# Splitting the score maxima on GpSimd, and turning them one step later, in two 512-key attentions

## The chip, the cores and the metric

The kernel runs on one core of one Trainium2 chip. The time is the device time of one execution of the whole program in microseconds, as the median of several runs. Three runs of the kernel before took 1183.32, 1192.98 and 1194.06 us; the median is 1192.98 us.

## The reference

The program is a decoder of two layers over x of 4 sequences x 512 tokens x 128 channels (16 heads of 8 channels). It adds six blocks to x one after the other: an RWKV recurrence, a small cross attention, a dense path with mixture-of-experts, an attention with relative positions, a latent cross attention, and an attention with register tokens and two groups of keys. Two of these hold a full softmax attention of 512 queries against 512 keys for 64 heads (4 sequences x 16), and the change touches these two alone. Cut to that:

```
# dense path of the first layer ("da", causal)
scores = einsum('bqhd,bkhd->bhqk', q, k) / sqrt(hd)
scores = where(causal, scores, finfo.min)
o = einsum('bhqk,bkhd->bqhd', softmax(scores), v)
# last block ("ga", grouped keys): token q sees the keys of its own group
l = where(key_mask, einsum('bqhd,bkhd->bhqk', q * scale, k), -inf)
x_pos / x_neg = einsum('bhqk,bkhd->bqhd', softmax(l), v)
```

## The kernel before, in words

Both attentions are one function, `attention_stage`, called with the tag `da` (causal) and the tag `ga` (not causal). The 64 heads are taken four at a time, which makes 16 **units** (`QUADS`), and a unit has 8 **steps**, so 128 steps (`STEPS`). q and k are held as sums of bfloat16 parts, so that the score matmuls run in bfloat16.

In step `s` each engine has its own fixed list of work, in program order, and semaphores alone tie the lists together.

- **Scores.** TensorE computes the scores of two heads for 128 queries, queries on partitions (`scores`, L947), into one of two pairs of PSUM banks. In `da` eight small matmuls lower the masked square (`mask_scores`, L958). VectorE takes the negated row maxima (L1196). The scores of step s wait for the reduction of step s-2.
- **Maxima.** After the eighth step of a unit VectorE splits the 128 x 16 maxima into three bfloat16 parts in four small dependent instructions (`split_maxima`, L1181 to L1187). In the second step of the next unit (`step % 8 == 1`) TensorE turns the parts onto 12 rows (`turn_maxima`, L969), ScalarE copies them from PSUM to `mrows` (`copy_maxima`, L1108), and SP, or ScalarE for the first unit, sends two small DMAs into rows of `qst` (`load_maxima`, L838).
- **Turned scores.** `S_LAG` steps after a step's scores, TensorE computes the scores again with keys on partitions (`scores_t`, L983); the rows loaded above subtract the maximum inside the matmul. The first of a unit (r == 0) waits for the two DMAs. `S_LAG` is 14 in `da` and 13 in `ga`. The results and the turned maxima share a ring of three PSUM banks (`st_ring`, `wait_bank`).
- **Exponentials.** ScalarE takes exp of both heads (L1100) into `pt`. In `da` GpSimd zeroes the masked triangle (`affine_select`, L897).
- **Values.** `V_LAG` = 3 steps later TensorE multiplies `pt` with the values (`values`, L1002) into one bank for the unit. When a unit's eight are done, ScalarE copies the bank out (`copy_output`, L1120), and the first value matmul of the next unit waits for that copy.

TensorE's order in a step of `da` is: turned scores, scores, mask, values, and in one step of eight the turn of the maxima. In `ga` it is: scores, turned scores, values, turn. ScalarE's order is: exponentials, copy of the maxima, copy of the output. SP issues, for unit u, the maxima's two DMAs and then the loads of unit u+3 (L820), in one queue. After step 127 come the sums over heads, reciprocals and the output projections (`join`, `densify`, `output`, L1015 to L1027), some of them at fixed steps of the drain.

Of the kernel before, what the change touches and what calls it, by code (L numbers as in the profile page):

```python
# [21 lines left out]
ALU = mybir.AluOpType  # L22
# [677 lines left out]
QUADS = B * H // 4  # L700
STEPS = 8 * QUADS


def attention_stage(nc, g, tag, xn, wq, wk, wv, group, scale, o, wo, take, patch=None, causal=False, classes=None,
# [3 lines left out]
    KT = KS + 3  # L708
    NBUF, SLOTS = 4, 3
    S_GROUPS, ST_BANK, ST_BANKS, O_BANK = 2, 4, 3, 7  # L710
    S_LAG, V_LAG = 14 if causal else 13, 3
    GATE_STEP, ROUTE_STEPS, LOGIT_STEP = 24, 8, 10

    def first_query(kt):
        return kt * 128 if causal else 0

    def keys_of(qt):
        return (qt + 1) * 128 if causal else T
# [11 lines left out]
    st_ring, st_slot, turn_slot = [], {}, {}  # L730
    for step in range(STEPS + S_LAG):
        t = step - S_LAG
        if t >= 0:
            for par in range(2):
                st_slot[t, par] = len(st_ring)
                st_ring.append(("scores", 2 * t + par + 1))
        if step % 8 == 1 and 8 < step < STEPS + 8:
            turn_slot[step // 8 - 1] = len(st_ring)
            st_ring.append(("maxima", step // 8))

    def st_bank(slot):
        return ST_BANK + slot % ST_BANKS

    with ExitStack() as ctx:
# [8 lines left out]
        with ExitStack() as inner:  # L753
            def isb(name, shape, dt=fp32):
                return inner.enter_context(nc.sbuf_tensor(f"{tag}_{name}", shape, dt))
# [3 lines left out]
            pt = isb("pt", [128, SLOTS, 4, T])  # L759
            zero = isb("zero", [128, T])  # L760
            nmax = isb("nmax", [128, 2, 2, 2, QT])
            mrest = isb("mrest", [128, 2, 2, 2, QT])
            mparts = isb("mparts", [128, 2, QT, 2, 3, 2], bf16)
            mrows = isb("mrows", [12, 2, T], bf16)
# [5 lines left out]
            m_loaded = [sem(f"m_loaded_{n}") for n in range(2)]  # L770
# [18 lines left out]
            with nc.Block() as block:  # L789
# [89 lines left out]
                @block.gpsimd  # L879
                def _(pool):  # L880
                    nc.gpsimd.memset(kst[32:64, :, :, :], 1.0).then_inc(ones_set, 1)
                    nc.gpsimd.memset(kst[96:128, :, :, :], 1.0).then_inc(ones_set, 1)
                    pool.wait_ge(ones_set, 2)
                    nc.gpsimd.memset(zero[:, :], 0.0).then_inc(zeroed, 1)
                    nc.gpsimd.memset(v9[:, :, :, HD:HD + 1], 1.0).then_inc(one, 1)
                    if gates:
                        gates.clear(pool)
                    if front:
                        front.gpsimd(pool)
                    if causal:  # L890
                        for t in range(STEPS):
                            u, r = divmod(t, 8)
                            kt, pr = divmod(r, 2)
                            q0 = first_query(kt)
                            pool.wait_ge(exped, 2 * t + 2)
                            square = pt[:, (4 * u + kt) % SLOTS, 2 * pr:2 * pr + 2, q0:q0 + 128]
                            nc.gpsimd.affine_select(square, square, [[0, 2], [1, 128]], ALU.is_ge, 0.0, base=0,  # L897
                                                    channel_multiplier=-1).then_inc(selected, 1)
                    if finish:
                        finish.add(pool)  # L900

                @block.tensor
                def _(pe):
# [126 lines left out]
                    for step in range(ALL_STEPS):  # L1030
                        t = step - S_LAG
                        if causal and 0 <= t < STEPS:
                            scores_t(t)
                        if step < STEPS:
                            scores(step)
                            if causal:
                                mask_scores(step)
                        if not causal and 0 <= t < STEPS:
                            scores_t(t)
                        if 0 <= t - V_LAG < STEPS:  # L1040
                            values(t - V_LAG)
                        if step % 8 == 1 and step // 8 - 1 in turn_slot:
                            turn_maxima(step // 8 - 1)
                        if front and step < S_LAG:
                            front.registers_pe(pe, step)
                        if gates and step < ROUTE_STEPS:
                            gates.route(pe, step)
                        if front and step == S_LAG - 1:
                            clear_output()
                        if step in OUT_STEP:  # L1050
                            output(OUT_STEP[step])
                        if step in JOIN_STEP:
                            join(JOIN_STEP[step])
                            densify(JOIN_STEP[step])
                        if gates and step == S_LAG - 1:
                            pe.wait_ge(gates.copied, 1)
# [12 lines left out]
                def _(act):  # L1069
# [34 lines left out]
                    def copy_maxima(u):  # L1104
                        act.wait_ge(m_turned, u + 1)
                        if u >= 2:
                            act.wait_ge(m_loaded[u % 2], 32 * (u // 2))
                        nc.scalar.activation(mrows[:, u % 2, :], g.ps[0:12, st_bank(turn_slot[u]), :], ACT.Identity)\  # L1108
                            .then_inc(m_ready, 1)
# [15 lines left out]
                    for step in range(ALL_STEPS):  # L1125
                        t = step - S_LAG
                        if front and step < S_LAG:
                            front.registers_act(act, step)
                        if 0 <= t < STEPS:
                            exponentials(t)  # L1130
                        if step % 8 == 1 and step // 8 - 1 in turn_slot:
                            copy_maxima(step // 8 - 1)
                            if step // 8 == 1:
                                load_first_maxima()
                        if gates and step == GATE_STEP + 6:
                            gates.exp(act)
                        p = t - V_LAG
                        if p >= 0 and p % 8 == 7:
                            copy_output(p // 8)
                        if finish and step == ALL_STEPS - 2:  # L1140
                            act.wait_ge(taken, 1)
                            finish.square(act)
# [12 lines left out]
                def _(dve):  # L1155
# [16 lines left out]
                    else:  # L1172
                        split()

                    def split_maxima(u):
                        dve.wait_ge(maxed, 8 * (u + 1))
                        if u >= 2:
                            dve.wait_ge(m_turned, u - 1)
                        n = u % 2
                        part = lambda k: mparts[:, n, :, :, k, :].rearrange("p q a r -> p a r q")  # L1180
                        nc.vector.tensor_copy(part(0), nmax[:, n]).then_inc(split1, 1)  # L1181
                        dve.wait_ge(split1, u + 1)
                        nc.vector.tensor_tensor(mrest[:, n], nmax[:, n], part(0), ALU.subtract).then_inc(split2, 1)
                        dve.wait_ge(split2, u + 1)
                        nc.vector.tensor_copy(part(1), mrest[:, n]).then_inc(split3, 1)
                        dve.wait_ge(split3, u + 1)
                        nc.vector.tensor_tensor(part(2), mrest[:, n], part(1), ALU.subtract).then_inc(split4, 1)  # L1187

                    chain = gates.chain(dve) if gates else None
                    for step in range(STEPS):  # L1190
                        u, r = divmod(step, 8)
                        pr, qt = divmod(r, 4)
                        if gates and (step == LOGIT_STEP or step >= GATE_STEP):
                            next(chain, None)
                        dve.wait_ge(scored, step + 1)
                        nc.vector.tensor_reduce(nmax[:, u % 2, :, pr, qt],  # L1196
                                                g.ps[:, 2 * (step % S_GROUPS):2 * (step % S_GROUPS) + 2, 0:keys_of(qt)],
                                                AX.X, ALU.max, negate=True).then_inc(maxed, 1)
                        if r == 7:
                            split_maxima(u)  # L1200
                        if front and step < S_LAG:
                            front.registers_dve(dve, step)

                    def invert(b):
                        dve.wait_ge(summed, b + 1)
# [1850 lines left out]
```

## Time and profile before

| what | value |
|---|---|
| median of three runs | 1192.98 us |
| profiled execution, its own time | 1189.37 us |
| its span in the trace | 1187.6 us |
| PE busy / DVE / ACT / POOL, share of the span | 92% / 68% / 61% / 29% |
| mean granted TensorE clock | 0.968 |
| stage `da`, steps 0 to 127 of the maxima | 156.2 to 296.5 us |
| stage `ga`, steps 0 to 127 of the maxima | 992.6 to 1154.9 us |

PE is TensorE's matmuls, PEld its weight loads, DVE VectorE, ACT ScalarE, POOL GpSimd, SP the queue that issues DMAs. Times in the views are microseconds from the start of the span. A row of the timeline merges neighbouring instructions of one line; "x8" is their number and the second figure the time from the first start to the last end. Brackets give the idle time of that engine before the row and what ended it.

### The profile page before, as it was taken

How to read it: one execution, taken by the hardware profiler on the slowest of the kernel's cores; microseconds unless marked ns; L12 is line 12 of the kernel's file. 1: busy time of each engine (PE TensorE's matmuls, PEld its weight loads, DVE VectorE, ACT ScalarE, POOL GpSimd, SP SyncE). 2: the span in 40 equal slices, each digit the busy share in tenths (PEclk: the TensorE clock that was granted, in tenths of full speed). 3: DMA queues.
4: the chain of work that ended last, by engine and by line, in shares of the span. 5: the costliest groups of instructions: out<-in, count | busy, mean ns of one | idle time of the engine just before them, and what ended most of it. 6: DMA issues, size and time to landing. Idle time of an engine off the chain costs nothing. (4 is left out here: it accounts for less than half of the span.)

```text
span 1187.6 us, 35597 instructions
## 1 busy us (share of the span) xinstructions
PE 1097.9 (92%) x14750; PEld 562.0 (47%) x14750; DVE 810.4 (68%) x1312; ACT 729.9 (61%) x1464; POOL 340.4 (29%) x667
## 2 busy tenths in 40 slices
PE   6999899999899998889999999999988888899997
PEld 2344443333244443567767767766745333222222
DVE  4897478888533443377767767777716466999995
ACT  5313637888554434466675766666744373899994
POOL 0552203333235244333333224322113431100000
PEclk9999869999999999899999999999989997999999
DMA  5000054211093200601021021101100003511100
GB/s 203 1 0 1 8 153 150 57 45 31 4 183 76 71 1 0 125 14 10 8 20 10 8 17 10 11 8 9 11 6 1 1 14 83 202 44 44 44 17 36
DMA packets 134927, 51.61 MB, mean 43 GB/s; under 512 B 103968, under 2 KB 126512, under 8 KB 134256
## 3 DMA queue, kind: packets, MB, share of 16 engines
q1 hardware_dynamic: 134732, 49.32, 17.8%
q8 instruction: 118, 1.93, 0.7%
q14 instruction: 41, 0.34, 0.1%
q10 hardware_dynamic: 36, 0.02, 0.0%
HBM read 33.09 MB, written 15.81 MB: 41 GB/s over the span
## 5 line engine op out<-in xcount | busy, mean ns | idle before, releaser
L2489 DVE TENSOR_REDUCE re_nmax<-ps 128x1 f32<-128x512 f32 x256 | 159.0, 683 | 57.9 <-PE ps L2292 57.9
L2423 ACT ACTIVATE normed<-ps,re_nmax 128x512 f32<-128x512 f32 x256 | 154.9, 693 | 4.7 <-DVE re_nmax L2489 4.7
L2313 PE MATMUL ps<-const,normed 128*128 128x128 f32 x1024 | 147.0, 283 | 2.5 <-ACT normed L2423 2.2
L1100 ACT ACTIVATE ga_pt<-ps 128x512 f32<-128x512 f32 x256 | 139.2, 598 | 15.4 <-PE ps L983 13.8
L2429 ACT ACTIVATE re_pT<-ps 128x512 f32<-128x512 f32 x128 | 76.6, 599 | 116.2 <-PE ps L2313 116.0
L1196 DVE TENSOR_REDUCE ga_nmax<-ps 128x2 f32<-128x1024 f32 x128 | 146.7, 1216 | 1.4 <-PE ps L947 1.4
L2313 PEld LDWEIGHTS ps<-const,normed 128*128 128x128 f32 x1024 | 110.4, 142 | 28.7 <-issue 14.9
L1196 DVE TENSOR_REDUCE da_nmax<-ps 128x2 f32<-128x256 f32 (+3 forms) x128 | 102.9, 821 | 20.7 <-PE ps L958 18.8
L1100 ACT ACTIVATE da_pt<-ps 128x512 f32<-128x512 f32 (+3 forms) x256 | 96.7, 435 | 31.6 <-PE ps L983 28.9
L2509 DVE COPY re_pT<-ps 128x512 f32<-128x512 f32 x128 | 82.5, 685 | 34.1 <-PE ps L2313 34.1
L1659 DVE TENSOR_TENSOR ex_u<-ps,ex_s 128x512 f32<-128x512 f32 x48 | 32.8, 690 | 90.9 <-PE ps L1494 68.0
L1002 PE MATMUL ps<-ga_pt,ga_v 128*9 128x256 f32 x1024 | 78.9, 381 | 8.4 <-ACT ga_osum L1120 8.4
L897 POOL TENSOR_SCALAR_AFFINE_SELECT da_pt<-da_pt 128x256 f32<-128x256 f32 x128 | 52.7, 412 | 114.7 <-ACT da_pt L1100 114.6
L2235 POOL TENSOR_TENSOR re_keys<-ff_xn,vec 128x64 f32<-128x64 f32 (+1 forms) x60 | 17.3, 288 | 219.7 <-PE ps L2292 219.6
L1578 ACT ACTIVATE ex_s<-ps 128x512 f32<-128x512 f32 x48 | 28.2, 597 | 78.8 <-PE ps L1494 78.8
L2282 PE MATMUL ps<-re_keys,re_qbd 32*128 32x512 f32 x512 | 75.5, 652 | 0.6 <-POOL re_qbd L2239 0.3
L1716 POOL TENSOR_TENSOR ex_u<-ex_u,ex_gates 128x512 f32<-128x512 f32 x32 | 45.0, 1416 | 82.8 <-DVE ex_u L1659 67.5
L2248 POOL TENSOR_TENSOR re_qrel<-wide,const 128x64 f32<-128x64 f32 x256 | 68.6, 300 | 0.0
L2360 PE MATMUL ps<-re_pT,re_v_far 128*9 128x128 f32 x1536 | 65.5, 286 | 2.6 <-ACT wide L2445 1.5
L1494 PE MATMUL ps<-ff_xn,weights 128*128 128x512 f32 x128 | 61.2, 601 | 0.0
L1002 PE MATMUL ps<-da_pt,v 128*9 128x256 f32 (+1 forms) x768 | 52.2, 347 | 4.7 <-POOL da_pt L897 3.9
L947 PE MATMUL ps<-ga_kst,ga_qst 50*128 50x512 bf16 x256 | 50.8, 394 | 6.1 <-DVE ga_nmax L1196 4.8
(398 smaller groups left out, 1983.9 us busy)
## 6 DMA issues: line engine op xcount, KB each, us to landing
ex_gates<-gates_scratch SPq DMA_DIRECT2D x4, 2048.0 KB, 15.9
da_qst<-da_stacks SPq DMA_DIRECT2D x32, 96.0 KB, 2.2
da_kst<-da_stacks SPq DMA_DIRECT2D x32, 96.0 KB, 2.3
ga_qst<-ga_stacks SPq DMA_DIRECT2D x32, 96.0 KB
ga_kst<-ga_stacks SPq DMA_DIRECT2D x32, 96.0 KB
da_stacks<-da_qkparts SPq DMA_DIRECT2D x6, 384.0 KB, 3.1
ga_stacks<-ga_qkparts SPq DMA_DIRECT2D x6, 384.0 KB, 2.7
weights<-in_weights SPq DMA_DIRECT2D x1, 2048.0 KB, 10.5
```

Source lines behind the costliest of these rows:

```text
L1002: last = nc.tensor.matmul(g.ps[32 * j:32 * j + HD + 1, O_BANK, lo:hi], v9[:, QT * b + kt, 4 * quad + j, :], pt[:, (4 * u + kt) % SLOTS, j, ...
L1100: nc.scalar.activation(pt[:, (4 * u + kt) % SLOTS, 2 * pr + par, q0:T], g.ps[:, st_bank(st_slot[t, par]), q0:T], ACT.Exp)\
L1196: nc.vector.tensor_reduce(nmax[:, u % 2, :, pr, qt], g.ps[:, 2 * (step % S_GROUPS):2 * (step % S_GROUPS) + 2, 0:keys_of(qt)], AX.X, ALU.ma ...
L1494: nc.tensor.matmul(g.ps[:, 2 * m + n % 2, :], g.w(w)[:, bass.ts(f, 128)], x[:, b, :], start=True, stop=True).then_inc(up, 1)
L2248: nc.gpsimd.tensor_tensor(qrel[:, m, pair, :, :, :, two], qd[:, b % 2, OCT * at:OCT * at + OCT, 4 * pair:4 * pair + 4].unsqueeze(2) .broad ...
L2282: nc.tensor.matmul(g.ps[:, S_BANK + quad, :], qbd[rows, m, :, :, :].rearrange("p o h c -> p (o h c)"), keys[rows, b % 2, m, :], start=True ...
L2313: last = nc.tensor.transpose(g.ps[:, bank_of("tile", s, idx), bass.ts(kt, 128)], p[:, QUAD_ORDER[idx], bass.ts(kt, 128)], g.c("ident"))
L2360: last = nc.tensor.matmul(far_out[32 * j:32 * j + HD + 1, :], values, weights, start=kt == 0, stop=kt == QT - 1)
L2423: nc.scalar.activation(p[:, QUAD_ORDER[idx], :], g.ps[:, S_BANK + QUAD_ORDER[idx], :], ACT.Exp, bias=nmax[:, s % 2, idx:idx + 1]).then_inc ...
L2429: nc.scalar.activation(pT_of(s, QUAD_ORDER[idx]), turned_of(s, idx), ACT.Identity)\
L2489: nc.vector.tensor_reduce(nmax[:, s % 2, idx:idx + 1], g.ps[:, S_BANK + quad, :], AX.X, ALU.max, negate=True).then_inc(maxed, 1)
L2509: nc.vector.tensor_copy(pT_of(s, QUAD_ORDER[idx]), turned_of(s, idx)).then_inc(dve_pT, 1)
```

## The change

The four splitting instructions move from VectorE to GpSimd, except for the first unit of `ga`, where VectorE keeps them. The turn of the maxima moves from the second to the third step of a unit, in both attentions. In `ga` `S_LAG` becomes 14, and VectorE instead of ScalarE copies the turned maxima out, after the reduction of the third step. In `da` ScalarE still does it, now in the third step. In `da` GpSimd's list is now: split of unit u, then the selection of the same step.

```diff
-    S_LAG, V_LAG = 14 if causal else 13, 3
+    S_LAG, V_LAG = 14, 3
...
-        if step % 8 == 1 and 8 < step < STEPS + 8:
+        if step % 8 == 2 and 8 < step < STEPS + 8:
             turn_slot[step // 8 - 1] = len(st_ring)
...
@@ list of GpSimd
+                    def split_maxima(u):
+                        pool.wait_ge(maxed, 8 * (u + 1))
+                        if u >= 2:
+                            pool.wait_ge(m_turned, u - 1)
+                        n = u % 2
+                        part = lambda k: mparts[:, n, :, :, k, :].rearrange("p q a r -> p a r q")
+                        nc.gpsimd.tensor_copy(part(0), nmax[:, n]).then_inc(split1, 1)
+                        pool.wait_ge(split1, u + 1)
+                        nc.gpsimd.tensor_tensor(mrest[:, n], nmax[:, n], part(0), ALU.subtract).then_inc(split2, 1)
+                        pool.wait_ge(split2, u + 1)
+                        nc.gpsimd.tensor_copy(part(1), mrest[:, n]).then_inc(split3, 1)
+                        pool.wait_ge(split3, u + 1)
+                        nc.gpsimd.tensor_tensor(part(2), mrest[:, n], part(1), ALU.subtract).then_inc(split4, 1)
...
+                    for step in range(STEPS + S_LAG):
+                        if step % 8 == 0 and (8 if causal else 16) <= step <= STEPS:
+                            split_maxima(step // 8 - 1)
+                        if causal and step >= S_LAG:
+                            select(step - S_LAG)
...
@@ list of TensorE
-                        if step % 8 == 1 and step // 8 - 1 in turn_slot:
+                        if step % 8 == 2 and step // 8 - 1 in turn_slot:
                             turn_maxima(step // 8 - 1)
...
@@ list of ScalarE
-                        if step % 8 == 1 and step // 8 - 1 in turn_slot:
-                            copy_maxima(step // 8 - 1)
+                        if step % 8 == 2 and step // 8 - 1 in turn_slot:
+                            if causal:
+                                copy_maxima(step // 8 - 1)
                             if step // 8 == 1:
                                 load_first_maxima()
...
@@ list of VectorE
+                    def copy_maxima(u):
+                        dve.wait_ge(m_turned, u + 1)
+                        if u >= 2:
+                            dve.wait_ge(m_loaded[u % 2], 32 * (u // 2))
+                        nc.vector.tensor_copy(mrows[:, u % 2, :], g.ps[0:12, st_bank(turn_slot[u]), :])\
+                            .then_inc(m_ready, 1)
...
                         dve.wait_ge(scored, step + 1)
+                        if r == 0 and u >= 2:
+                            dve.wait_ge(split4, u - 1)
                         nc.vector.tensor_reduce(nmax[:, u % 2, :, pr, qt],
                                                 g.ps[:, 2 * (step % S_GROUPS):2 * (step % S_GROUPS) + 2, 0:keys_of(qt)],
                                                 AX.X, ALU.max, negate=True).then_inc(maxed, 1)
-                        if r == 7:
-                            split_maxima(u)
+                        if not causal and step == 7:
+                            split_first_maxima()
+                        if not causal and r == 2 and u >= 1:
+                            copy_maxima(u - 1)
...
+                    if not causal:
+                        copy_maxima(QUADS - 1)
```

## Rows read from the trace of the kernel before

**Rows 1.** Busy time by stretch: da, then ga; PE, PEld, DVE, ACT, POOL, clock, DMA
```profile
240.00:280.00 40.00, 38.48 (x716) 15.49 (x708) 34.51 (x56) 32.77 (x87) 15.74 (x39) 1.00 0.19 53
...
1080.00:1120.00 40.00, 37.45 (x406) 11.27 (x408) 39.45 (x49) 38.20 (x73) 0.00 (x0) 1.00 0.16 44
```
**Rows 2.** Waits in ga, 1000 to 1156 us: in total, times, longest
```profile
PEld ps L947 <- DVE ga_nmax L1196: 37.2, 88, 1.2
...
PE ps L1002 <- ACT ga_osum L1120: 7.7, 14, 0.7
```
**Rows 3.** The chain that ended last, in ga: start, length, what
```profile
1104.40 0.61 ACT ga_osum L1120
...
1114.37 0.61 ACT ga_osum L1120
```
**Rows 4.** Timeline of VectorE in ga, the eight reductions of one unit
```profile
1065.93 9.14 DVE L1196 TENSOR_REDUCE ga_nmax<-ps 128x2 f32<-128x1024 f32 x8
```
**Rows 5.** Timeline of TensorE in ga around the change of unit
```profile
1064.11 0.39 PE L947 MATMUL ps<-ga_kst,ga_qst 50*128 50x512 bf16 x2
...
1065.26 0.62 PE L1002 MATMUL ps<-ga_pt,ga_v 128*9 128x256 f32 x8 [0.54 <-ACT ga_osum L1120]
...
1065.81 0.39 PE L947 MATMUL ps<-ga_kst,ga_qst 50*128 50x512 bf16 x2
...
1067.21 0.39 PE L947 MATMUL ps<-ga_kst,ga_qst 50*128 50x512 bf16 x2
...
1068.47 0.39 PE L947 MATMUL ps<-ga_kst,ga_qst 50*128 50x512 bf16 x2
...
1069.56 0.39 PE L947 MATMUL ps<-ga_kst,ga_qst 50*128 50x512 bf16 x2
```
**Rows 6.** Timeline in da, one unit: from the first values to the first turned scores
```profile
221.74 0.62 PE L1002 MATMUL ps<-da_pt,v 128*9 128x256 f32 x8 [0.28 <-POOL da_pt L897]
...
222.17 0.39 PE L969 MATMUL ps<-identb,da_mparts 128*12 128x128 bf16 x4
...
222.49 0.28 PE L983 MATMUL ps<-da_qst,da_kst 51*128 51x256 bf16 x2
222.59 0.59 ACT L1108 ACTIVATE da_mrows<-ps 12x512 bf16<-12x512 f32 x1 [0.23 <-PE ps L969]
...
222.99 0.60 PE L1002 MATMUL ps<-da_pt,v 128*9 128x256 f32 x8
...
223.20 1.47 SPq L838 DMA_DIRECT2D da_qst<-da_mrows  x2
...
223.52 0.28 PE L983 MATMUL ps<-da_qst,da_kst 51*128 51x256 bf16 x2
...
226.03 0.39 PE L983 MATMUL ps<-da_qst,da_kst 51*128 51x512 bf16 x2
```
**Rows 7.** Line 838 alone: duration of one issue, ns min/median/max
```profile
L838 SPq DMA_DIRECT2D da_qst<-da_mrows x30: 695/702/913, 179.5 to 299.6; - x30
```
**Rows 8.** Timeline in da, third unit: issue, and what waits for it
```profile
188.87 1.50 SPq L838 DMA_DIRECT2D da_qst<-da_mrows  x2
...
191.60 0.39 PE L983 MATMUL ps<-da_qst,da_kst 51*128 51x512 bf16 x2 [0.35 <-DMA da_qst<-da_mrows]
```
**Rows 9.** Timeline of VectorE in da, the splits of two neighbouring units
```profile
220.93 0.20 DVE L1181 CAST da_mparts<-da_nmax 128x16 bf16<-128x16 f32 x1
...
229.31 0.20 DVE L1181 CAST da_mparts<-da_nmax 128x16 bf16<-128x16 f32 x1
```
**Rows 10.** Groups by line and shape: busy us, mean ns of one, idle before
```profile
L1196 DVE TENSOR_REDUCE ga_nmax<-ps 128x2 f32<-128x1024 f32 x128 | 146.7, 1216 | 1.4 <-PE ps L947 1.4
...
L2248 POOL TENSOR_TENSOR re_qrel<-wide,const 128x64 f32<-128x64 f32 x256 | 68.6, 300 | 0.0
...
L1716 POOL TENSOR_TENSOR ex_u<-ex_u,ex_gates 128x512 f32<-128x512 f32 x32 | 45.0, 1416 | 82.8 <-DVE ex_u L1659 67.5 <-DMA ex_gates<-gates_scratch 15.1
...
L2799 DVE COPY ga_pt<-ps 128x512 f32<-128x512 f32 x4 | 2.7, 684 | 0.0
```

More of the change, by code:

```diff
@@ L889, in _, with select @@
                         front.gpsimd(pool)
[L890 to L898, printed above, removed]
+                    def split_maxima(u):
[11 more added lines that the diff above has]
+                        nc.gpsimd.tensor_tensor(part(2), mrest[:, n], part(1), ALU.subtract).then_inc(split4, 1)
+                    def select(t):
+                        u, r = divmod(t, 8)
+                        kt, pr = divmod(r, 2)
+                        q0 = first_query(kt)
+                        pool.wait_ge(exped, 2 * t + 2)
+                        square = pt[:, (4 * u + kt) % SLOTS, 2 * pr:2 * pr + 2, q0:q0 + 128]
+                        nc.gpsimd.affine_select(square, square, [[0, 2], [1, 128]], ALU.is_ge, 0.0, base=0,
+                                                channel_multiplier=-1).then_inc(selected, 1)
+                    for step in range(STEPS + S_LAG):
[3 more added lines that the diff above has]
+                            select(step - S_LAG)
                     if finish:
@@ L1173, in _, with split_first_maxima @@
                         split()
[L1175 to L1179, printed above, removed]
+                    def split_first_maxima():
+                        dve.wait_ge(maxed, 8)
+                        n = 0
                         part = lambda k: mparts[:, n, :, :, k, :].rearrange("p q a r -> p a r q")
                         nc.vector.tensor_copy(part(0), nmax[:, n]).then_inc(split1, 1)
-                        dve.wait_ge(split1, u + 1)
+                        dve.wait_ge(split1, 1)
                         nc.vector.tensor_tensor(mrest[:, n], nmax[:, n], part(0), ALU.subtract).then_inc(split2, 1)
-                        dve.wait_ge(split2, u + 1)
+                        dve.wait_ge(split2, 1)
                         nc.vector.tensor_copy(part(1), mrest[:, n]).then_inc(split3, 1)
-                        dve.wait_ge(split3, u + 1)
+                        dve.wait_ge(split3, 1)
                         nc.vector.tensor_tensor(part(2), mrest[:, n], part(1), ALU.subtract).then_inc(split4, 1)
                     chain = gates.chain(dve) if gates else None
+                    def copy_maxima(u):
[4 more added lines that the diff above has]
+                            .then_inc(m_ready, 1)
                     for step in range(STEPS):
```

## The prediction, made before the changed kernel ran

> **What bounds the kernel now.** I read first the busy time by stretch, because the change touches two stages that need not have the same limit. In the causal attention (`da`) the reader should see PE at 38.5 of 40 us, VectorE at 34.5 and ScalarE at 32.8; in the grouped one (`ga`) VectorE at 39.45 of 40, ScalarE at 38.2 and PE at 37.45 [rows 1]. So in `ga` VectorE is full, and ScalarE nearly is; in `da` it is PE that is never idle for long.
>
> Busy time alone doesn't say what a relieved VectorE brings in `ga`. The waits there show that PE waits 37.2 us for the maxima, but also 14 times, once per unit, for ScalarE's copy of the output [rows 2]. In the chain that ended last the same copy comes back every 1114.37 - 1104.40 = 9.97 us, the length of a unit of `ga` [rows 3]. Two chains lie side by side, and I work out each.
>
> VectorE's: eight reductions take 9.14 us and the last lasts 1.216, so they start every (9.14 - 1.216) / 7 = 1.13 us [rows 4, 10]. Eight are 9.05, and the rest of the unit, 9.97 - 9.05 = 0.92 us, is the split.
>
> PE's: its scores start 1.09 us apart when nothing holds it; around the change of unit the distances are 1.70 (the values wait for the output copy), 1.40 (the turn stands in it) and 1.26 (the turn took a slot of the bank ring, so the next turned scores wait for a newer exponential) [rows 5]. Those three and five of 1.09 make 9.81. The missing 0.16 is VectorE's, and an estimate is that 0.12 of it falls in the step just ahead of the wait for the output copy. That copy is timed by ScalarE's exponentials and not by the maxima, so it gives nothing back. PE with ScalarE would need 9.93 us by itself.
>
> In `da` the thing to read is the way from the turn to the first turned scores of the unit. The turn starts at 222.17, ScalarE's copy at 222.59 for 0.59 us, the pair of DMAs at 223.20 [rows 6]. One issue lasts 0.70 [rows 7], so the second of the pair starts 1.47 - 0.70 = 0.77 later. How long it then takes to land is seen where PE waited for it: 188.87 + 1.50 - 0.70 = 189.67 to 191.60, which is 1.93 us [rows 8]. In the steady unit that gives 223.20 + 0.77 + 1.93 = 225.90, and the matmul that needs it starts at 226.03 [rows 6]. It is hidden by 0.13 us, no more.
>
> **The change, part by part.**
>
> *The turn one step later in `da`.* `S_LAG` stays 14 there, so from turn to first use five steps become four. Values to the next turned scores take 223.52 - 222.99 = 0.53, turned scores to values 0.50, values to turn 222.17 - 221.74 = 0.43, and the turn 222.49 - 222.17 = 0.32 [rows 6]. From the values at 221.74 the new order is 222.27, 222.77, turn at 223.20, next turned scores at 223.52. So PE is where it was before, but the turn is 1.03 us later. The copy starts 0.42 after it, at 223.62, and ends at 224.21. SP's first issue follows at 224.23, the second at 225.00, and it lands at 226.93. PE stands in order, its turned scores come first in the step, and everything behind them (scores, mask, values) waits: 226.93 - 226.03 = **0.90 us per unit**. It doesn't come back later, because the way closes on itself: first turned scores, two steps on to the new unit, turn, copy, landing. The unit goes from 8.38 [rows 9] to about 9.28. VectorE, ScalarE and GpSimd stand behind PE and drain meanwhile.
>
> Ten units run at the steady length: 9.0 us. The first five are longer than 8.38 for other reasons (half clock, the writes of the parts in SP's queue, the gates on VectorE). The third already waits for its rows [rows 8], but its pair is issued late behind those writes, and a later copy swallows that. I take 0.6 each, 3.0, between 0 and 1.03. The last unit's rows are needed only after the first sums over heads; nothing. Sum for `da` +12.0. The ends: 0, if something in the loop gives way, and 16, if the unit-loads, now issued right behind the pair, delay it by 0.25 as well.
>
> The Trainium skill ("DMA: Bandwidth & Descriptors", Anatomy of one DMA) puts about 2.0 us of fixed cost on a DMA however small. Rows 8 show 1.93. By the page the landing would be 0.07 later and `da` would pay an estimated 13 us.
>
> *The split on GpSimd.* Four small dependent instructions. The trace has none of 16 elements there; the nearest, 128x64, lasts 0.30, and 128x512 up to 1.42 [rows 10]. I take 0.35 with the semaphore, 1.4 in all, since 16 is near 64. In `da` the last maximum is ready at 220.93 [rows 9] and the new turn starts at 223.20, so 2.27 us are there, 0.57 per instruction; nothing. Without that cover each 0.1 more costs 0.4 per unit. The selection queued behind the split on GpSimd is late by about a microsecond, and the values that need it come in the fourth step, ahead of the new wait, which hides it; nothing, at most 0.3 per unit if I am wrong on that.
>
> *VectorE without the split in `da`.* It is busy 34.5 of 40 [rows 1] and waits for PE; nothing. The first units with the gates could gain up to 0.9 each, which the new wait takes back.
>
> *`ga`: VectorE loses the split and gains the copy.* A copy of 512 PSUM elements lasts 0.684 and, like the reductions, overlaps its neighbour by 1.216 - 1.13 = 0.085, so it costs 0.60 [rows 4, 10]. VectorE's chain becomes 9.65. PE's and ScalarE's stays at 9.93: the output copy, the turn and the ring slot all shift by one step together, and ScalarE's copy of the maxima was not on it. So a unit gives 9.97 - 9.93 = 0.04, some 15 of them 0.6. The ends are 0 and 0.32. Turn to first use stays four steps there, and the copy comes about as soon after the turn as ScalarE's did, so no new DMA wait; an estimate from 9.93 leaves 0.2 us of room.
>
> *`S_LAG` 14 in `ga`.* The drain is one step longer, PE's 1.09 [rows 5]: +1.1. In the ramp ScalarE now waits for VectorE's copy before it issues the first unit's two DMAs, with part of the front queued behind it: +0.3, between -0.5 and 1.
>
> **Sum**: 12.0 - 0.6 + 1.1 + 0.3 = +12.8 us on the profiled execution's 1189.37, which gives 1202.2. The median of the runs lies 3.6 us above that execution; from it the same sum gives 1205.8. I say 1204, and move the rivals by the same 1.8. What this kernel's measurement can tell from no change is about 1%, 11.9 us.
>
> **Rivals.**
> - *`ga` falls to VectorE's floor* (0.14). For it: PE's waits for the maxima are much the longest [rows 2]. Against it: the output copy's place in the chain [rows 3]. A unit would be 9.65, 15 x 0.32 = 4.8 instead of 0.6: 1200.
> - *`da` absorbs half of the wait* (0.12), because the late writes and loads in SP's queue had lengthened the landing I measured in the third unit. Against it: in the steady unit PE would then have had more than 0.13 of room, which I can't see. 6 less: 1198.
> - *VectorE decides in both stages, faster* (0.10). The split stands between a unit's last maximum and the next unit's first, and PE's scores wait for maxima two steps back. If that is what times `da` too, each of its 15 units loses 0.92, and `ga`'s 0.32: -13.8 - 4.8 + 1.1 gives 1174. It decides if the rows land before PE asks for them, 0.9 us sooner than I have them. Against it: VectorE's 14% of idle time in `da` [rows 1].
> - *The split is late* (0.08). If a small GpSimd instruction takes 0.70 with its semaphore instead of 0.35, the split ends 0.5 after the turn's place, 15 x 0.5 on top: about 1212.
>
> **How the numbers follow.** The forecast has 0.56; its own range is 1199 to 1209, and about two thirds of it lie above the 1%. Slower 0.56 x 0.65 + 0.08, rounded to 0.45; within 1% 0.56 x 0.35 + 0.14 + 0.12, rounded to 0.45; faster 0.10. The range 1188 to 1213 leaves out the faster rival and the ends.
>
> **What would show it.** In the changed trace of `da`: a wait of PE's turned scores for the maxima's DMA in nearly every unit, 0.7 to 1.0 us each; units of 9.2 to 9.4; the turn about 1.03 later against the values before it. No such wait, with units of 8.4 or less, makes the prediction wrong. In `ga`: VectorE no longer full, the wait for the output copy still there each unit, units of 9.9; units of 9.65 or less are the first rival. On GpSimd: four instructions of 0.2 to 0.4 that end before the turn; a turn that waits for them is the last rival.

## The result

The changed kernel takes 1204.27 us (1199.52 to 1207.41, four runs) against 1189.62 us for the kernel before, run beside it (1183.32 to 1194.06). The ratio is 1.013, 95% interval 1.0084 to 1.0176. It is slower, by 10 to 21 us; whether by more than 1% is left open by the interval's lower end. The forecast was 1204, from a sum of +12.8 us. The medians differ by 14.7.

The profiled execution has a span of 1205.2 us, 17.6 more than before. The groups of the changed kernel's waits between 160 and 320 us (the causal attention) say where most of it is. The last line here, PE's wait for the maxima's DMA, is the one to compare; the second fence has it for the kernel before, between 160 and 300 us:

```profile
DVE da_nmax L1224 <- PE ps L978: 46.9, 88, 1.8
...
PEld ps L1003 <- DMA da_qst<-da_mrows: 14.0, 14, 1.0
PE ps L1003 <- DMA da_qst<-da_mrows: 12.8, 15, 1.2
```
```profile
PE ps L983 <- DMA da_qst<-da_mrows: 1.2, 3, 0.5
```

One unit of it in the timeline, the counterpart of [rows 6]:

```profile
228.01 0.62 PE L1022 MATMUL ps<-da_pt,v 128*9 128x256 f32 x8 [0.28 <-ACT wide L1140]
...
228.56 0.28 PE L1003 MATMUL ps<-da_qst,da_kst 51*128 51x256 bf16 x2
...
229.06 0.60 PE L1022 MATMUL ps<-da_pt,v 128*9 128x256 f32 x8
...
229.49 0.39 PE L989 MATMUL ps<-identb,da_mparts 128*12 128x128 bf16 x4
...
229.81 0.28 PE L1003 MATMUL ps<-da_qst,da_kst 51*128 51x256 bf16 x2
229.91 0.59 ACT L1128 ACTIVATE da_mrows<-ps 12x512 bf16<-12x512 f32 x1 [0.37 <-PE ps L989]
...
230.52 1.47 SPq L838 DMA_DIRECT2D da_qst<-da_mrows  x2
...
233.22 0.39 PE L1003 MATMUL ps<-da_qst,da_kst 51*128 51x512 bf16 x2 [0.84 <-DMA da_qst<-da_mrows]
```

From the first values to the turn are 1.48 us, 0.43 before. From the pair's first issue to the matmul are 2.70, and with 0.77 to the second issue the landing takes 1.93, the value of [rows 8] again. PE waits for the last 0.84 of it. Ahead of it stands GpSimd's split, from the timeline of that engine:

```profile
227.22 0.25 POOL L897 CAST da_mparts<-da_nmax 128x16 bf16<-128x16 f32 x1 [0.19 <-DVE da_nmax L1224]
227.56 0.23 POOL L899 TENSOR_TENSOR da_mrest<-da_nmax,da_mparts 128x16 f32<-128x16 f32 x1
227.85 0.25 POOL L901 CAST da_mparts<-da_mrest 128x16 bf16<-128x16 f32 x1
228.19 0.27 POOL L903 TENSOR_TENSOR da_mparts<-da_mrest,da_mparts 128x16 bf16<-128x16 f32 x1
```

It lasts 1.24 us and ends 1.03 before the turn. In the grouped attention the chain that ended last still returns through the output copy, now every 9.94 us instead of 9.97 [rows 3]. VectorE is no longer full: the second fence is its timeline, with idle time ahead of the third reduction and the new copy taking 1106.67 - 1106.07 = 0.60 of its list. PE still waits for the output copy at a unit's first values (third fence):

```profile
1103.19 0.61 ACT ga_osum L1140
...
1113.13 0.61 ACT ga_osum L1140
```
```profile
1104.93 1.23 DVE L1224 TENSOR_REDUCE ga_nmax<-ps 128x2 f32<-128x1024 f32 x1 [0.21 <-PE ps L967]
1106.07 0.67 DVE L1213 CAST ga_mrows<-ps 12x512 bf16<-12x512 f32 x1
1106.67 7.99 DVE L1224 TENSOR_REDUCE ga_nmax<-ps 128x2 f32<-128x1024 f32 x7
```
```profile
1113.88 0.62 PE L1022 MATMUL ps<-ga_pt,ga_v 128*9 128x256 f32 x8 [0.67 <-ACT ga_osum L1140]
```

**The length of each stage** is read from its 128 reductions. Each row gives the start of the first and of the last, first for the changed kernel, then for the one before:

```profile
L1224 DVE TENSOR_REDUCE da_nmax<-ps x128: 410/823/1227, 156.4 to 309.9; 128x2 f32<-128x256 f32 x32, 128x2 f32<-128x512 f32 x32, 128x2 f32<-128x768 f32 x32, 128x2 f32<-128x1024 f32 x32
L1224 DVE TENSOR_REDUCE ga_nmax<-ps x128: 1202/1204/1227, 1006.3 to 1170.8; 128x2 f32<-128x1024 f32 x128
```
```profile
L1196 DVE TENSOR_REDUCE da_nmax<-ps x128: 411/818/1227, 156.2 to 295.3; 128x2 f32<-128x256 f32 x32, 128x2 f32<-128x512 f32 x32, 128x2 f32<-128x768 f32 x32, 128x2 f32<-128x1024 f32 x32
L1196 DVE TENSOR_REDUCE ga_nmax<-ps x128: 1205/1216/1227, 992.6 to 1153.6; 128x2 f32<-128x1024 f32 x128
```

The causal stage is 153.5 us (139.1 before), the grouped one 164.5 (161.0 before). The second difference, 3.5, is not what it seems; the runs below tell it apart.

### The profile page after: what moved, and what is told of

Read it like the earlier page. It is cut to its first block and busy times, and to the rows that moved or that the text cites. A ratio compares the mean times of both kernels' runs of the same rounds, so it can differ in the third digit from the quotient of the medians.

```text
span 1205.2 us, 35625 instructions
## 1 busy us (share of the span) xinstructions
PE 1103.2 (92%) x14750; PEld 564.5 (47%) x14750; DVE 796.6 (66%) x1204; ACT 722.8 (60%) x1448; POOL 369.0 (31%) x791
## 3 DMA queue, kind: packets, MB, share of 16 engines
q8 instruction: 118, 1.93, 0.7%
## 5 line engine op out<-in xcount | busy, mean ns | idle before, releaser
L2345 PEld LDWEIGHTS ps<-const,normed 128*128 128x128 f32 x1024 | 110.5, 142 | 28.6 <-issue 14.7
L1003 PE MATMUL ps<-da_qst,da_kst 51*128 51x512 bf16 (+3 forms) x256 | 50.4, 314 | 13.3 <-DMA da_qst<-da_mrows 12.8
L1003 PE MATMUL ps<-ga_qst,ga_kst 53*128 53x512 bf16 x256 | 57.0, 390 | 0.6 <-DMA ga_qst<-ga_mrows 0.5
```

The lines of the kernel that those rows point to most:

```text
L1003: last = nc.tensor.matmul(g.ps[:, st_bank(st_slot[t, par]), q0:T], kst[rows, u % NBUF, pr, bass.ts(kt, 128)], qst[rows, u % NBUF, pr, q0:T ...
L2345: last = nc.tensor.transpose(g.ps[:, bank_of("tile", s, idx), bass.ts(kt, 128)], p[:, QUAD_ORDER[idx], bass.ts(kt, 128)], g.c("ident"))
```

## The experiments

The theory: in the causal attention the maxima's DMAs, one step later, land 0.9 us after PE asks, once per unit; all else is small. The rivals: GpSimd's work, or the grouped attention's ramp and drain, carries a good part. The table has each run's stages from the same rows as above, the unit being the distance of the turns, steady part. Units and stages come from one trace each; ratios come from all runs of a kernel.

| run | ratio to before (95%) | causal: unit, stage | grouped: unit, stage |
|---|---|---|---|
| before | 1 | 8.39, 139.1 | 9.97, 161.0 |
| after | 1.013 (1.0084 to 1.0176) | 9.32, 153.5 | 9.94, 164.5 |
| da_new_only | 1.0098 (1.0064 to 1.0133) | 9.32, 153.4 | 9.97, 165.1 |
| ga_new_only | 0.9983 (0.996 to 1.0007) | 8.39, 141.3 | 9.94, 160.2 |
| da_turn1 | 1.0015 (0.9992 to 1.0039) | 8.46, 140.6 | 9.94, 164.2 |
| da_two_queues | 1.0124 (1.0085 to 1.0162) | 9.31, 154.3 | 9.93, 164.2 |
| da_lag15_b | 1.0017 (0.9992 to 1.0041) | 8.44, 140.8 | 9.94, 164.1 |
| da_turn_first_b | one run | 8.89, 147.2 | 9.94, 164.2 |
| da_split_dve_b | one run | 9.32, 154.3 | 9.94, 162.7 |
| ga_early_out_b | 1.0111 (1.0071 to 1.015) | 9.32, 153.6 | 9.70, 159.5 |
| best_ga | 0.9986 (0.9959 to 1.0014) | 8.39, 140.0 | 9.70, 161.0 |
| best_both | 0.9986 (0.9965 to 1.0008) | 8.53, 141.3 | 9.70, 161.7 |

### One attention at a time

`da_new_only` and `ga_new_only` take the change's branch by `causal`; for the turn, for example:

```diff
-                        if step % 8 == 2 and step // 8 - 1 in turn_slot:
+                        if step % 8 == TURN and step // 8 - 1 in turn_slot:
```

> The causal attention as in the changed kernel, the grouped one as in the kernel before (split on VectorE, turn in the second step, copy on ScalarE, lag 13). Theory (the maxima's DMAs land too late in the causal attention): units of 9.32 us there and nearly the whole loss, +13 to +14 us against the kernel before, units of 9.97 in the grouped one. Rival (the grouped attention's ramp and longer drain carry a good part): +9 to +10 us.

> The grouped attention as in the changed kernel, the causal one as before. Theory: units of 9.94 instead of 9.97 save 0.4 us, the drain costs 1.1 and the ramp about 2.5, together +2 to +4 us. Rival (VectorE's relief in the grouped attention is worth something): a gain of 2 to 5 us.

The causal part alone costs 1.0098, some 11.7 us of 1189.66. That lies between the theory's 13 to 14 and the rival's 9 to 10, and the interval (7.6 to 15.8 us) takes in both, so the total doesn't decide between them; the causal stage of 153.4 us and its unit of 9.32, both as in the changed kernel, do. The grouped part alone can't be told from nothing, and is if anything a gain of 2 us where I had expected a loss of 2 to 4. Its rival, that VectorE's relief is worth 2 to 5 us, can't be excluded by the total, but the unit gives only 0.03. The parts of the grouped change were not run one by one.

These two also explain the grouped stage's 3.5 us. It lasts 165.1 us with the old code (`da_new_only`) and 160.2 with the new (`ga_new_only`), so it is not the code. The stretch of 34 us from its first reduction, in the changed kernel and then in `ga_new_only` (PE, PEld, DVE, ACT, POOL, granted clock, DMA share, GB/s):

```profile
1006.20:1040.20 34.00, 28.92 (x158) 12.41 (x158) 28.58 (x34) 14.37 (x28) 7.26 (x12) 0.70 0.31 97
```
```profile
990.30:1024.30 34.00, 26.90 (x202) 12.01 (x202) 32.28 (x37) 18.65 (x37) 8.26 (x16) 0.90 0.40 128
```

The clock was granted at 0.70 of full speed in one and 0.90 in the other; the kernel before had 0.90 in its own first 34 us of this stage. The other runs with this same grouped code line up with it: 0.80 and 162.7 us (`da_split_dve_b`), 0.75 and 164.2 (`da_turn_first_b`), 0.70 and 164.1 to 164.2 (three runs). At equal clock the new code is a little shorter than the old: 160.2 against 161.0 at 0.90, 164.2 against 165.1 (`da_new_only`) at 0.75. The stretches at the lower level (1.2 GHz instead of 2.4) fall differently from run to run. At the start of the causal stage they do so too; these are 20 us each, first of the kernel before, then of the changed one, then of `ga_new_only` (same columns):

```profile
156.00:176.00 20.00, 18.76 (x206) 10.36 (x201) 13.03 (x21) 2.76 (x6) 0.46 (x2) 0.59 0.55 168
176.00:196.00 20.00, 18.90 (x326) 7.58 (x325) 16.61 (x33) 15.26 (x41) 7.38 (x18) 0.90 0.43 143
```
```profile
156.00:176.00 20.00, 18.02 (x180) 10.86 (x178) 11.04 (x15) 0.79 (x2) 1.00 (x4) 0.53 0.56 169
176.00:196.00 20.00, 18.23 (x280) 7.02 (x280) 13.19 (x18) 13.28 (x35) 8.25 (x24) 0.79 0.31 104
```
```profile
156.00:176.00 20.00, 18.67 (x188) 11.05 (x188) 11.65 (x19) 1.08 (x3) 0.00 (x0) 0.53 0.56 170
176.00:196.00 20.00, 19.09 (x298) 7.12 (x292) 15.24 (x27) 13.82 (x37) 6.61 (x16) 0.79 0.34 114
```

`ga_new_only` has the causal code of before, 2.2 us more than it in this stage (141.3), and the changed kernel's clock of 0.53 and 0.79. Against that run the changed causal attention costs 153.5 - 141.3 = 12.2 us.

### The causal attention: how much of the wait is bought back

```diff
# da_turn1: turn in the second step, split still on GpSimd
+    TURN = 1 if causal else 2
...
-                        if step % 8 == 2 and step // 8 - 1 in turn_slot:
+                        if step % 8 == TURN and step // 8 - 1 in turn_slot:
# da_lag15_b: five steps from the turn to the first use again
-    S_LAG, V_LAG = 14, 3
+    S_LAG, V_LAG = 15 if causal else 14, 3
# da_turn_first_b: in the third step, but ahead of its values
+                        turns = step % 8 == 2 and step // 8 - 1 in turn_slot
+                        if turns and causal:
+                            turn_maxima(step // 8 - 1)
                         if 0 <= t - V_LAG < STEPS:
                             values(t - V_LAG)
-                        if step % 8 == 2 and step // 8 - 1 in turn_slot:
+                        if turns and not (causal):
                             turn_maxima(step // 8 - 1)
```

> The changed kernel, but in the causal attention the maxima are turned in the second step again; the split stays on GpSimd, the lag 14. Theory: the split ends 1.3 us after the last reduction, about when the turn's place comes, so the unit returns to 8.4 to 8.6 us, 11 to 13 us faster than the changed kernel. Rival (the work on GpSimd, split or the selections behind it, is what costs): units stay above 9.

> The changed kernel with S_LAG 15 in the causal attention, so from the turn in the third step to the first turned scores there are five steps again. Theory: the wait for the maxima's DMAs is gone, units of 8.4 to 8.5 us, 11 to 13 us faster than the changed kernel, less 1 us for a longer drain. Rival (the later turn collides with something else in the third step, or the GpSimd work costs): units stay above 9.

> The changed kernel, but in the causal attention the turn of the third step stands ahead of that step's values. The turn then starts 0.43 us sooner against the values before it. Theory: the way from turn to landing is the loop's, so the unit shortens by about that, from 9.32 to 8.85 to 8.95 us. Rival (the wait replaces another that ends at the same time): 9.3.

All three come out as the theory says. With the turn back in its step, or the first use one step on, units are 8.46 and 8.44, and 13 us are gone (the medians are 1190.48 and 1190.96). PE's wait for the maxima's DMA is gone with them: the first line is of the changed kernel between 200 and 310 us, the second of `da_lag15_b` in the same window, and `da_turn1` has the same 0.3 between 200 and 300.

```profile
PE ps L1003 <- DMA da_qst<-da_mrows: 10.1, 12, 0.9
```
```profile
PE ps L1003 <- DMA da_qst<-da_mrows: 0.3, 1, 0.3
```

The longer lag was to cost 1 us in the drain; a ratio of 1.0017 with an interval up to 1.0041 can't show that. Half the distance gives half the effect: 8.89, and the wait in the timeline of `da_turn_first_b` is 0.41 instead of 0.84:

```profile
230.98 0.39 PE L1003 MATMUL ps<-da_qst,da_kst 51*128 51x512 bf16 x2 [0.41 <-DMA da_qst<-da_mrows]
...
239.86 0.39 PE L1003 MATMUL ps<-da_qst,da_kst 51*128 51x512 bf16 x2 [0.40 <-DMA da_qst<-da_mrows]
```

In `da_turn1` the turn waits for GpSimd's split for a moment: it starts 0.50 to 0.51 after the first values instead of 0.43, which is the 0.07 by which its unit is longer than 8.39.

### The split on VectorE, the turn in the third step

```diff
-                        if not causal and step == 7:
-                            split_first_maxima()
+                        if (causal and r == 7) or (not causal and step == 7):
+                            split_maxima(u)
```

> The changed kernel, but in the causal attention VectorE does the split as before; the turn stays in the third step. Theory: the split is not on the way in either place, units of 9.3 us. Rival (GpSimd's split or the selections it delays cost time): units of 9.1 or less.

9.32, the same to the hundredth, and PE's wait for the maxima's DMA between 200 and 310 us is 10.1 us in 12 waits, as in the changed kernel. Where the split is done doesn't matter in the causal attention while the turn stands in the third step. The rival that GpSimd's work is what costs falls.

### The pair of DMAs from two queues

```diff
+                            elif causal:
+                                n = step // 8 - 1
+                                act.wait_ge(m_ready, n + 1)
+                                act.dma_start(qst[64 + KS:64 + KT, n % NBUF, :, :], mrows[6:12, n % 2, :])\
+                                    .then_inc(m_loaded[n % 2], 16)
```

> The changed kernel, but in the causal attention ScalarE issues the second of each pair of maxima DMAs, right after its copy, instead of SP 0.77 us after the first. Theory: the pair lands 0.7 us sooner, so a unit takes 8.6 to 8.7 us, 9 to 10 us faster than the changed kernel, unless ScalarE's 0.7 us of issuing comes into its own way. Rival (the wait at the first turned scores only takes the place of another that ends at the same time): units stay at 9.3.

My expectation was wrong, and the reservation at the end of its theory is what came. The wait for the DMA is gone, and another of the same length stands in its place, two steps earlier. ScalarE's issue of 0.73 us holds up its exponentials, which have to free the bank that PE needs next. First PE's waits between 200 and 310 us, then the timeline:

```profile
PE ps L1003 <- ACT da_pt L1120: 10.3, 12, 1.1
```
```profile
229.70 0.72 SPq L838 DMA_DIRECT2D da_qst<-da_mrows  x1
229.70 0.73 ACTq L1159 DMA_DIRECT2D da_qst<-da_mrows  x1
...
230.47 1.15 ACT L1120 ACTIVATE da_pt<-ps 128x256 f32<-128x256 f32 x4 [0.80 <-ACT da_mrows L1128]
...
230.91 0.23 PE L1003 MATMUL ps<-da_qst,da_kst 51*128 51x128 bf16 x1 [0.83 <-ACT da_pt L1120]
```

The units stay at 9.31, so by its total this run speaks neither for the theory nor for its rival; only the trace tells them apart.

### What sets the unit in the grouped attention

```diff
                                 .then_inc(exped, 1)
+                            if par == 0 and early_copy(t):
+                                copy_output((t - V_LAG) // 8)
...
-                        if p >= 0 and p % 8 == 7:
+                        if p >= 0 and p % 8 == 7 and not early_copy(t):
                             copy_output(p // 8)
```

> The changed kernel, but in the grouped attention ScalarE copies a unit's output between the two exponentials of the step instead of after both. Theory (the wait of the next unit's first values for that copy sets the unit, not VectorE): the copy comes 0.4 to 0.5 us sooner, and the unit falls from 9.94 to VectorE's own 9.65 to 9.75 us, 3 to 4 us in all. Rival (the unit is set by something else, the copy's wait only stands where the slack is): 9.94.

The unit falls from 9.94 to 9.70 by a reordering on ScalarE alone, though VectorE's work is the same. PE's wait for the copy is 0.33 in the timeline of this kernel, where it was 0.67 in the changed one:

```profile
1079.89 0.62 PE L1022 MATMUL ps<-ga_pt,ga_v 128*9 128x256 f32 x8 [0.33 <-ACT ga_osum L1145]
```

So with the split gone from VectorE, the output copy was what held the unit; and once that wait is shorter, VectorE's 9.65, the figure of the first rival, is nearly reached. The total doesn't show it, since the interval (1.0071 to 1.015) overlaps that of the changed kernel; the stages do at equal clock: 159.5 us here against 162.7 in `da_split_dve_b`, both at 0.80.

### Two combinations meant to be faster

> The causal attention as in the kernel before (split on VectorE, turn in the second step), the grouped one as in the changed kernel, with its output copy between the two exponentials. Theory: units of 8.39 and 9.70 us; against the kernel before 15 x 0.27 = 4 us less, plus 0.3 for the longer drain: 1184 to 1187, a ratio of 0.996 to 0.998. Rival (the grouped gain is lost in the ramp or in clock): 1.000 or more.

> As best_ga, and the output copy between the two exponentials in the causal attention too. In the trace of the kernel before PE waits 0.28 us per unit for that copy there. Theory: units of 8.1 to 8.3 us in the causal attention if nothing else ends at the same time, 1 to 4 us less than best_ga; but the maxima's DMAs had only 0.13 us of room, so a gain there may come back as a wait for them. Rival: units of 8.39 or longer, since the second exponential comes 0.5 us later and the next turned scores and GpSimd's selection wait for it.

`best_ga` joins the causal attention of before with the changed grouped one and the earlier copy. It is clearly faster than the changed kernel; against the kernel before, 0.9986 with an interval over 1 shows no difference, although its grouped unit is 0.27 shorter. Its grouped stage came out at 161.0 us, as before, but with a granted clock of 0.75 in its first 34 us instead of 0.90. Against `da_turn_first_b` with the same 0.75 it is 3.2 us shorter, and against the old grouped code at 0.75 (`da_new_only`) 4.1, near the 15 x 0.27 = 4.05 expected. So the gain is there, of the size of the clock's differences in the ramp, and too small for the totals. `best_both` adds nothing to it. In the changed kernel PE waits 0.28 for ScalarE's copy at a unit's first values (the timeline above). My expectation had that wait in the kernel before as well, but there [rows 6] put the 0.28 down to GpSimd's selection. The wait for the copy is nearly gone here, once in 90 us, and the unit is 8.53 instead of 8.39. From its waits between 210 and 300 us:

```profile
PEld ps L1004 <- ACT da_pt L1124: 16.3, 54, 0.4
...
PEld ps L990 <- DVE da_mparts L1214: 2.3, 10, 0.2
PE ps L1023 <- ACT wide L1146: 0.3, 1, 0.3
```

PE now waits at the turn for VectorE's split, and it waits for exponentials ahead of its turned scores. The 0.14 may come from either, from the split or from the later second exponential; neither was tried alone, so its cause stays open.

## Why the prediction was right

- **The turn one step later in the causal attention**: 0.90 us per unit forecast, 9.32 - 8.39 = 0.93 measured; +12.0 for the stage forecast, 12.2 measured against `ga_new_only`, which had the same granted clock in the ramp. By the distances of the turns in these two traces the last ten gave 9.0 and the first five 3.5, forecast 9.0 and 3.0. The 1.93 us of landing, taken from a unit where PE waited, held to the hundredth, and the three runs that give back a whole, a whole and a half of the distance bear out the mechanism.
- **The landing's size**: the trace shows 1.93 again, in units where nothing else is late. The Trainium skill ("DMA: Bandwidth & Descriptors", Anatomy of one DMA) puts about 2.0 us of fixed cost on a DMA issued from GpSimd; these two are issued from SP, which the prediction did not say. By 2.0 the estimate was 13 us; the trace agrees to 0.07.
- **The split on GpSimd**: 1.4 us forecast, 1.24 measured, hidden. Right, and the rival of a late split falls. So do the rival that the causal attention absorbs half of the wait, and the one in which VectorE decides in both stages, which would have shortened the causal unit; it grew by 0.93.
- **The grouped unit**: 9.93 forecast, 9.94 measured. The rival of VectorE's floor at 9.65 falls for this change; it became true only when the output copy was moved.
- **The drain**: +1.1 was mis-sized. From the last reduction to the end of the span it is 0.4 more (34.4 against 34.0 us; `da_new_only`, with the old lag, has 34.0 too). Why most of the added step hides was not tried.
- **The ramp**: +0.3 had the wrong sign, though inside its range of -0.5 to 1. Where the clock was the same, the grouped stage of `ga_new_only` is 160.2 against 161.0, which with 15 x 0.03 for the units leaves about -0.3.
- **What the sum lacked**: the clock. Of the 17.6 us between the two profiled executions some 6.5 go with the clock that each drew at the start of its stages: 14.4 - 12.2 = 2.2 in the causal one, and 164.5 - 160.2 = 4.3 in the grouped one. That leaves 11.1 for the change, against the sum's 12.8. Parts that the change doesn't touch move by as much: from the last causal reduction to the first grouped one it is 697.3 us before, 692.3 in `ga_new_only` and 693.5 in `best_ga`, with the same program there. How much of this is in the median difference of 14.7 can't be said; the sum's 12.8 lies inside the interval (10 to 21 us).
- **Luck**: that 1204 meets 1204.27 is in part chance. It was the middle between two starting points, the profiled execution and a median of three runs; from the median of four, 1189.62, the same sum gives 1202.4.

## What to carry to other kernels

A step that is moved takes its whole latency along: measure how long before its first use the result lands, and if that room is smaller than a step, the difference is paid once per loop, whatever engine was relieved. When an engine is full but the period also closes through a second chain (here exponentials, output copy, next values), work out that chain's own length before hoping for anything from the relief; here 0.3 us less per unit on the full engine (the split's 0.92 off, the copy's 0.60 on) gave 0.03. And a DMA issue took 0.7 us of the issuing engine's time here, so that moving it to an engine on the chain swapped one wait for another.

## What the runs showed of the hardware

Stretches at half clock at the start of a stage fell differently in runs of the same code: the first 34 us of the grouped stage had a granted clock of 0.90, 0.80, 0.75 or 0.70, and the stage was 160.2, 162.7, 164.2 or 164.1 to 164.5 us with the same program there. What decides which one a run gets, these runs don't show. The spread is more than the 0.24 us per unit of the earlier copy gave in 15 units. Four dependent GpSimd instructions of 128x16 took 0.23 to 0.27 us each and 1.24 in all, against 0.92 of VectorE's list before.
